# Four low-rank weight folds between two attentions: full-height matmuls, or four 32-row tiles side by side

## The reference, cut to what matters

```python
def _lora(t, down, up, alpha):
    return t @ down @ up * (LORA_W * alpha[0] / RANK)
q_in = x @ Wq + _lora(x, q_down, q_up, q_alpha)
org_ctx = context[:, :end, :]
ipa_ctx = context[:, end:, :]
k_in = org_ctx @ Wk + _lora(org_ctx, k_down, k_up, k_alpha)
v_in = org_ctx @ Wv + _lora(org_ctx, v_down, v_up, v_alpha)
out = _attention(q_in, k_in, v_in)
ipa_k = ipa_ctx @ Wk_ipa
ipa_v = ipa_ctx @ Wv_ipa
out = out + IPA_SCALE * _attention(q_in, ipa_k, ipa_v)
return out @ Wo + bo + _lora(out, o_down, o_up, o_alpha)
```

## Time and profile before

| what | value |
|---|---|
| median of three runs | 506.51 us (506.22, 506.51, 508.09) |
| the profiled execution | 506.04 us |
| its span, first to last instruction | 504.3 us |
| TensorE busy | 477.5 us, 95% |
| VectorE, ScalarE, GpSimd busy | 357.4, 292.7, 235.7 us |
| stretch of the seam, 99.6 to 129.4 us | 29.8 us |

### The profile page before, as it was taken

One profiled execution on the slowest core, in us unless ns is written; L12 is line 12 of the kernel. 1 busy time (PEld: TensorE's weight loads), 2 busy tenths in 40 slices (PEclk: granted clock), 3 DMA queues, 4 the chain that ended last, 5 costly groups with the idle time before them and its releaser, 6 DMA issues.

```text
span 504.3 us, 13570 instructions
## 1 busy us (share of the span) xinstructions
PE 477.5 (95%) x5109; PEld 376.4 (75%) x5113; DVE 357.4 (71%) x992; ACT 292.7 (58%) x1000; POOL 235.7 (47%) x331
## 2 busy tenths in 40 slices
PE   3999999999999999999999999799989999999996
PEld 2576666747678877888778777688757897899995
DVE  6788999787686668666686665857867779535553
ACT  3666656555676677666777657665674445513332
POOL 6664635145366554475544755233331990081430
PEclk9999999999999999999999999999999999999999
DMA  8900000000001110011000000022201200010001
GB/s 229 238 9 3 3 3 3 3 7 1 4 2 34 33 36 6 29 34 34 4 3 1 3 3 3 0 66 66 65 1 51 78 1 1 2 41 4 2 1 43
DMA packets 21872, 14.48 MB, mean 29 GB/s; under 512 B 5928, under 2 KB 21136, under 8 KB 21808
## 3 DMA queue, kind: packets, MB, share of 16 engines
q1 hardware_dynamic: 20704, 13.31, 9.9%
q10 hardware_dynamic: 1104, 0.30, 0.3%
HBM read 12.30 MB, written 1.05 MB: 26 GB/s over the span
## 4 chain that ended last, share of the span: by engine, by line
PE 69%; DVE 11%; issue 8%; POOL 5%; ACT 4%; DMA 1%; DVEq 0%; POOLq 0%
PE bank L1814 10%; PE bank L1758 6%; PE bank L1585 5%; PE bank L1823 5%; PE bank L1578 5%; PE bank L1565 5%; PE bank L1537 5%; PE bank L1490 5%; PE bank L1548 4%; PE bank L1557 4%; PE bank L1830 3%; POOL work L459 2%; ACT work L1184 2%; DVE work L792 2%; DVE negmax L782 2%
## 5 line engine op out<-in xcount | busy, mean ns | idle before, releaser
L497 POOL TENSOR_TENSOR work<-work,rsum 128x496 f32<-128x496 f32 x64 | 64.2, 1014 | 122.2 <-DVE rsum L798 122.2
L1184 ACT ACTIVATE work<-bank,negmax 128x124 f32<-128x124 f32 x256 | 90.4, 392 | 52.4 <-DVE ipa_s L784 52.3
L532 POOL TENSOR_SCALAR work<-work,slot 128x128 f32<-128x128 f32 x64 | 50.3, 801 | 44.6 <-DVE slot L873 25.7
L1184 ACT ACTIVATION_READ_ACCUMULATOR work<-bank,negmax 128x1 f32 x256 | 60.1, 235 | 0.0
L1814 PE MATMUL bank<-work 128*128 128x256 f32 x224 | 53.4, 381 | 0.0
L1333 ACT ACTIVATE work<-bank 128x256 f32<-128x256 f32 x64 | 24.6, 385 | 40.8 <-PE bank L1814 30.3
L1033 DVE SCALAR_TENSOR_TENSOR work<-work,bank 128x256 f32<-128x256 f32 x64 | 26.9, 420 | 28.7 <-ACT work L1333 28.3
L305 DVE TENSOR_TENSOR x_all<-bank,x_all 128x128 f32<-128x128 f32 x16 | 4.7, 292 | 56.8 <-PE bank L1758 54.8
L480 POOL TENSOR_TENSOR work<-work 128x512 f32<-128x512 f32 (+2 forms) x48 | 39.3, 818 | 11.8 <-DVE work L754 9.3
L629 DVE TENSOR_REDUCE work<-bank 128x8 bf16<-128x1024 f32 x32 | 39.0, 1220 | 7.6 <-PE bank L1375 7.2
L1814 PEld LDWEIGHTS bank<-work 128*128 128x128 f32 x224 | 40.3, 190 | 4.7 <-DVE work L1036 0.2
(11 more groups left out here) (199 smaller groups left out, 1104.0 us busy)
## 6 DMA issues: line engine op xcount, KB each, us to landing
work<-in_L_ffn_w_dram SPq DMA_DIRECT2D x42, 128.0 KB, 2.4
x_all<-in_x_dram SPq DMA_DIRECT2D x4, 256.0 KB, 5.9
out_dram<-x_all SPq DMA_DIRECT2D x4, 256.0 KB, 2.5
ctx_all<-in_ctx_dram SPq DMA_DIRECT2D x4, 192.0 KB, 6.0
ctx_all<-in_L_ffn_w_dram SPq DMA_DIRECT2D x6, 128.0 KB, 2.2
work<-in_L_xattn_Wq_dram SPq DMA_DIRECT2D x1, 512.0 KB, 6.5
work<-in_L_xattn_Wo_dram SPq DMA_DIRECT2D x1, 512.0 KB, 8.5
work<-in_L_ffn_We_dram SPq DMA_DIRECT2D x1, 512.0 KB, 6.6
```

The costliest lines, as they stand in the source:

```text
L497: pool.tensor_tensor(part, part, rsum1[:, b % 2, CH * n:CH * n + CH].unsqueeze(2).broadcast_to((128, CH, ORG)), ALU.mult).then_inc(Z.norm, 1)
L532: ins = pool.tensor_scalar(ohw_of(e)[:, k, :], count[:, :], slot[:, h, 0, k, e % E1:e % E1 + 1], slot[:, h, 1, k, e % E1:e % E1 + 1], ALU. ...
L1184: ins = act.activation(p1[:, b % 2, n, c, 0:ORG], blocks(bank[n])[:, c, 0:ORG], ACT.Exp, bias=negmax1[:, b % 2, h:h + 1], accum_out=sums1[ ...
```

## The change

The up matrices of o, q, k and v now lie under each other in one tile `ups` (rows 0, 32, 64, 96), the turned down matrices in the same rows of `downT`. `ext`, and the extra 32 rows of `wk1` and `wv1`, are gone. `fold_half(n)` makes half n of all four additions: three matmuls of 32 rows x 512 columns in row groups 1, 2 and 3 and four of 128 columns in row group 0, each into a bank of its own. VectorE adds all eight results to the weights (`added(n, name)`, semaphore `W.half` for ready, `W.added` for done); ScalarE's `take(0)` to `take(3)` fall away. `down_o_turn(0)` follows `down_turn` at b = 15, `down_o_turn(1)` stands at b = 16, `fold(6)` at b = 18. The loads change only in where the up matrices are put.

```diff
-            return slice(0, RANK) if n == 0 else slice(C, C + RANK)
-
-        FOLD_BANK = (0, 4, 5, 6, 0, 4, 0, 1, 2, 3, 4)
-        KEYS_TAKEN, VALUES_TAKEN, IPA_K_TAKEN, ALL_TAKEN = 2, 4, 5, 7
-        QUERIES_ADDED, ALL_ADDED = 2, 4
+            return slice(RANK * n, RANK * n + RANK)
+
+        O_ROWS = down_rows(0)
+        HALF_BANK = ({"q": 5, "k": 4, "v": 6, "o": 1}, {"v": 5, "q": 4, "k": 6, "o": 1})
+        HALF_ADDED = ({"q": 1, "k": 2, "v": 3, "o": 4}, {"v": 5, "q": 6, "k": 7, "o": 8})
+        FOLD_BANK = {6: 0, 7: 0, 8: 2}
+        IPA_K_TAKEN, ALL_TAKEN, ALL_ADDED = 1, 3, 8
...
-            def added(s, n):
-
-                to = (wq1[:, 512 * n:512 * n + 512], wo1[:, 4 * n:4 * n + 4, :].rearrange("p c n -> p (c n)"))[s >= 9]
-                dve.wait_ge(W.made, s + 1)
-                dve.tensor_tensor(to, bank[FOLD_BANK[s]][:, :], to, ALU.add).then_inc(W.added, 1)
+            def added(n, name):
+
+                part = slice(512 * n, 512 * n + 512)
+                rows = C if name in "kv" else D
+                to = wo1[:, 4 * n:4 * n + 4, :].rearrange("p c n -> p (c n)") if name == "o" else \
+                    {"q": wq1, "k": wk1, "v": wv1}[name][0:rows, part]
+                dve.wait_ge(W.half, 4 * (n + 1))
+                dve.tensor_tensor(to, bank[HALF_BANK[n][name]][0:rows, :], to, ALU.add).then_inc(W.added, 1)
...
-                if b == -1:
-                    added(9, 0)
-                    added(10, 1)
...
-                if b == 17:
-                    head_input(1)
-                if b == 18:
-                    added(4, 0)
-                    added(5, 1)
                 if b >= 17:
                     ffn_statistics(b - 17)
+                    added(b - 17, "qv"[b - 17])
                     xn1_of(b - 17)
+                if b == 17:
+                    added(0, "k")
+                    added(0, "v")
+                    head_input(1)
+                    added(0, "o")
+                if b == 18:
+                    added(1, "q")
+                    added(1, "k")
+                    added(1, "o")
...
-                act.wait_ge(made.ext, 1)
-                for n, to in enumerate((downT[:, 0, :], ext[C:C + RANK, 0, :], ext[C:C + RANK, 1, :])):
-                    rows = down_rows(n)
-                    act.activation(to, blocks(bank[0])[rows, n, 0:(D, C, C)[n]], ACT.Copy, scale=alpha[rows, n:n + 1])\
+                for n in range(3):
+                    rows, width = down_rows(1 + n), (D, C, C)[n]
+                    act.activation(downT[rows, 0, 0:width], blocks(bank[0])[rows, n, 0:width], ACT.Copy, scale=alpha[rows, n:n + 1])\
                         .then_inc(W.downT, 1)
 
             def down_o_turned(n):
 
                 act.wait_ge(W.turned, 2 + n)
-                act.activation(downT[:, 1 + 4 * n:5 + 4 * n, :], blocks(bank[(1, 6)[n]], RANK), ACT.Copy,
-                               scale=alpha[0:RANK, 3:4]).then_inc(W.downT, 1)
+                act.activation(downT[O_ROWS, 4 * n:4 * n + 4, :], blocks(bank[0])[O_ROWS, :, :], ACT.Copy,
+                               scale=alpha[O_ROWS, 3:4]).then_inc(W.downT, 1)
...
-                act.wait_ge(W.made, s + 1)
+                act.wait_ge(W.made, s - 5)
                 got_w = bank[FOLD_BANK[s]]
-                if s < 4:
-                    w, n = (wk1, wv1)[s // 2], s % 2
-                    to, got_w = w[0:C, 512 * n:512 * n + 512], got_w[0:C, :]
-                elif s == 6:
+                if s == 6:
...
                     down_turned()
+                    down_o_turned(0)
+                if b == 16:
+                    down_o_turned(1)
                 if b >= 16:
                     weighted(b - 16, bank[2])
-                if b == 16:
-                    take(0)
-                if b == 17:
-                    take(1)
-                    take(2)
-                    take(3)
                 if b == 18:
+                    take(6)
                     inputs(0)
-                    down_o_turned(0)
-                    down_o_turned(1)
...
+            def fold_half(n):
+
+                part = slice(512 * n, 512 * n + 512)
+                for r, (name, cols) in enumerate((("q", D), ("k", C), ("v", C))):
+                    rows = down_rows(1 + r)
+                    pe.matmul(bank[HALF_BANK[n][name]][0:cols, :], downT[rows, 0, 0:cols], ups[rows, part], start=True, stop=True)\
+                        .then_inc(W.half, 1)
+                for c in range(4):
+                    mm = pe.matmul(blocks(bank[HALF_BANK[n]["o"]])[:, c, :], downT[O_ROWS, 4 * n + c, :], ups[O_ROWS, 0:D],
+                                   start=True, stop=True)
+                mm.then_inc(W.half, 1)
...
                     pe.wait_ge(W.taken, IPA_K_TAKEN + 1)
+                    pe.wait_ge(W.added, ALL_ADDED)
...
-                if b == 0:
-                    pe.wait_ge(W.added, ALL_ADDED)
+                if b == -1:
+                    pe.wait_ge(W.added, HALF_ADDED[1]["q"])
...
-                    pe.wait_ge(W.added, ALL_ADDED - 1)
+                    pe.wait_ge(F.ys1, 3)
...
-                    pe.wait_ge(W.downT, 5)
+                    pe.wait_ge(W.added, HALF_ADDED[1]["k"])
                 if there(f):
                     keys(f, 0, *((Z.p_sb, CH * t + 2) if there(t) else (Z.v_sb, 2 * f)))
-                if b == -1:
-                    pe.wait_ge(W.added, QUERIES_ADDED)
-                    fold(6)
...
+                    pe.wait_ge(W.taken, IPA_K_TAKEN)
...
-                    pe.wait_ge(F.ys1, 3)
-                    fold(9)
-                    pe.wait_ge(Z.q_sb, 2)
-                    fold(10)
...
                     down_turn()
+                    down_o_turn(0)
                 if b == 16:
-                    pe.wait_ge(W.downT, 3)
-                    fold(0)
+                    pe.wait_ge(W.downT, 4)
+                    down_o_turn(1)
                 if b == 17:
                     pe.wait_ge(A.exp, 2 * B)
-                    fold(1)
-                    fold(2)
-                    fold(3)
+                    pe.wait_ge(A.o, B)
+                    pe.wait_ge(W.downT, 5)
+                    fold_half(0)
                 if b == 18:
-                    pe.wait_ge(W.taken, 2)
-                    fold(4)
-                    fold(5)
+                    fold(6)
+                    pe.wait_ge(W.added, 4)
+                    fold_half(1)
                     pe.wait_ge(A.x_new, B)
                     inputs(0)
-                    pe.wait_ge(A.o, B)
-                    down_o_turn(0)
-                    pe.wait_ge(W.taken, 4)
-                    down_o_turn(1)
-            pe.wait_ge(W.added, QUERIES_ADDED)
+            pe.wait_ge(W.added, HALF_ADDED[1]["v"])
```

40 lines of the change are left out of this document (13 added, 27 removed).

## The result

The changed kernel took 511.33 us (median of five executions, 508.14 to 511.95), the kernel before beside it 508.09 (506.22 to 508.52): ratio 1.0065, 95% interval 1.0044 to 1.0085. The forecast was 507.3, within 0.5% of before, and the range ended at 509.8; the result lies above it. The profiled execution took 510.95 us with a span of 509.1, 4.8 more than the 504.3 of before.

What follows compares the result with a forecast made beforehand. TensorE, busy 29.75 of the seam's 29.80 us, was taken as the bound. Its work, -5.3 us, plus waits of 2.05, 2.35, 0.8, 0.65 and 0.55 gave about +1.05 on 506.04: forecast 507.3 us, range 505.0 to 509.8.

Steps and rivals of the forecast that it cites:

- The folds and the tiles: TensorE in the seam: folds removed save 7.40 us, two fold_half at 1.05 add 2.1, net -5.3 us.
- the tiles don't overlap: At fold_half: tiles run one after the other, 3.4 us each, giving 509.4 to 510.8 us; chance 6%.
- TensorE's work decides: In the seam: VectorE and ScalarE keep up, 5.3 us gained, 500.7 us (503.9 with half the waits); chance 8%.
- Step 1: Ahead of ffn(1): TensorE waits for ScalarE's weighted(0), behind the copy of down_o_turn(1); idle 2.05 us.
- Step 3: Ahead of fold_half(1): TensorE waits until VectorE has added all four results of fold_half(0); idle 2.35 us.
- Step 4: Ahead of head_turn: TensorE waits for VectorE to add the first result of half 1; idle 0.8 us.
- Step 6: In ffn(3)'s second half: TensorE waits for ScalarE's weighted(3), with fold(6) gone from between; idle 0.55 us.
- Step 5: Ahead of ffn(3): TensorE waits for VectorE's first routing step, behind xn1_of(1) and three adds; idle 0.65 us.
- The sum: At scores(0, 0): -5.3 us of TensorE's work plus five waits, +1.1 us, the same as the walk's +1.05.
- the third rival: Idle 2.35 us ahead of fold_half(1) lowers the clock; half rate to ffn(3) adds 4.6 us, 511.7; chance 5%.
- signs of being wrong: First or second gap missing, a fold_half over 1.5 us, or the shift at scores(0, 0) not that at the end.
- Carried 1:1: From scores(0, 0) to the kernel's end: everything hangs on those scores, so the +1.05 us shift carries through in full.

Runs made afterwards that it cites:

- e12: Changed kernel with idle matmuls cut to the gaps: one ahead of ffn(1), two ahead of fold_half(1), two in round 12; 507.23 us, ratio 1.0007.
- e10: Kernel before with two idle matmuls filling TensorE's 1.45 us wait in round 12 of the second attention; 506.45 us, ratio 0.9986.
- e7: Changed kernel with VectorE's fourth add, added(0, o), put ahead of head_input(1); 508.94 us, ratio 1.0019.
- e6: Changed kernel with weighted(0) ahead of down_o_turned(1), fold(7) and fold(8) moved ahead of fold_half(1), and the fourth add ahead of head_input(1); 505.84 us, ratio 0.9965.
- e8: Kernel before with TensorE made to wait for two idle ScalarE copies behind fold(5), 1.38 us idle; 510.51 us, ratio 1.0066.
- e11: e6 with the idle matmuls of round 12 besides; 505.78 us, ratio 0.9976.
- e2: Changed kernel with four idle matmuls ahead of fold_half(1) only, the gap ahead of ffn(1) left idle; 508.39 us, ratio 1.0022.
- e3: Changed kernel with ScalarE's weighted(0) put ahead of down_o_turned(1); 506.53 us, ratio 0.9998.
- e4: Kernel before with TensorE made to wait for three idle ScalarE copies behind fold(5), 2.04 us idle; 511.66 us, ratio 1.0067.
- e1: Changed kernel with seven idle matmuls: three ahead of ffn(1), four ahead of fold_half(1); 508.60 us, ratio 1.0027.
- e5: Changed kernel with weighted(0) ahead of down_o_turned(1), and fold(7) and fold(8) moved ahead of fold_half(1); 506.35 us, ratio 0.9978.

## Why the prediction was wrong, point by point

**What bounds the seam** held: TensorE was full, and work taken from it came back as waits for ScalarE and VectorE.

**The folds and the tiles** held. The tiles overlap: a fold_half takes 1.11 us, predicted 1.05. Of the rivals, *the tiles don't overlap* (3.4 us each) is out, and so is *TensorE's work decides*: the 5.3 us were not gained.

**The waits** were found in the right places, with the right releasers, each somewhat too long. Step 1: 1.77 measured, 2.05 predicted. Step 3: 2.09 and 2.35. Step 4, with the clock kept (e12): 0.65 and 0.8. Step 6: 0.34 and 0.55. Step 5's wait is not marked in e12; the distance from L1560 to ffn(3) is 1.20 us (120.70 to 121.90) against 0.98 before, so 0.2 and not 0.65. A likely reason is that I counted from the starts of instructions and added about 0.1 us for each handover on top of durations that already hold some of it.

**The sum** of +1.05 us was right in sign and a little large: with the clock held, +0.43 at the first scores in one profile and +0.78 by the medians of e12 and e10. That e12 measures 507.23 us where 507.3 was forecast is partly luck: its 0.78 stands on 506.45 (e10), the forecast's 1.05 on the 506.0 to 506.5 known then. What the Trainium skill says of reading PSUM (TensorEngine Tiling (Array Packing), "PSUM Bottleneck") agrees with the traces in part: VectorE's adds, not the tiles, set when fold_half(1) may start (2.09 us). But the adds are only 2.6 of the 5.0 us that VectorE needs; the wait is as much a matter of what stands between them, for it is 0.91 with one add moved ahead (e7) and gone with other work in it as well (e6).

**The reading of the earlier trace rows** as the lower of TensorE's two levels is not what the granted clock says: the table by windows of before has 1.00 from 16 to 20 us, though two passes take 0.64 us there. What the lower level does to lengths is shown by the changed kernel instead, at 0.50 (1.12 us for 0.60).

**The step that failed** is the clock, which the sum put at nothing and the third rival at 5%. *The clock falls in the gap* was written down with its place, its mechanism and its price. It is what happened, in the gap ahead of fold_half(1), and it costs 3.6 of the 4.05 us that the seam lost. That the rival's 511.7 us lies so near the measured 511.33 is largely luck: it stands for +5.65 (1.05 + 4.6) on 506.04, where the seam lost 4.05 (0.43 + 3.62) and the two medians differ by 3.24. (Three of the five executions of before beside it, at 508.09 and more, lie where the later ones with a mean clock of 0.996 lie.) The price of 4.6 also rests on half rate for the work up to ffn(3); in the profile the lower clock stands longer, for some 10 us, and costs less, since part of it falls where TensorE would have waited anyway: the waits of steps 5 and 6 are not in that profile. The 5% had no ground. The earlier trace rows are one execution with 1.45 us of idle time and no fall, and the prediction itself says that they don't show what 2.35 us does. One of the three times that I had (506.22 to 508.09) lies where later executions with a mean clock of 0.996 lie, and I did not ask why. e7's profile shows that the very gap of the earlier trace rows can lower the clock, and by e8's mean clocks 1.38 us at the seam does it in most executions. The range ended at 509.8 since it left out this rival. None of the prediction's own signs of being wrong came true, for none of them asks for the clock.

**Carried 1:1** held for the loss (4.79 of 4.8 us of span), and not for a gain: e11 gives part of its 2.77 us back.

Open: why a gap lowers the clock in one execution and not in the next, why the 1.77 us ahead of ffn(1) lowered it in none of the three profiles that have them (the changed kernel, e2, e7) while 2.1 us did, and why it stays low for some 3.5 us in e3 and e7 and for some 10 in e4 and the changed kernel. Nor is it the same moment: by the table in steps of half a microsecond it falls in the middle of the gap in e4 (at 115.2, the gap ending at 116.1), but 0.9 us behind the gap's end in the changed kernel, 1.4 behind it in e7 and 1.7 in e3. The Trainium skill (TensorE: Matmul & The Clock Gate, Part 1) says that what watches TensorE's activity runs freely and does not restart with the kernel; by that the same gap would meet it at another moment in every execution, which fits the two groups of before and these moments, but no run here tests it. Open too is the one execution of the changed kernel at 508.14 us, whose mean clock (0.991) is as low as that of the others; there is no trace of it.

## What to carry to other kernels

An idle time of 1.4 to 2.1 us on a full TensorE could cost more than itself here: up to about 4 us more, by the granted clock behind it, and in some places and executions nothing more. So before folding work away from a saturated TensorE, look which waits that work was hiding, and put other needed work into the gap (e6) rather than leave it empty, watching where the next gap opens (1.86 us in e11); even idle matmuls were better than nothing (e1, e2, e12). And look at the granted clock of several executions, not of one: a gap that one profile shows to be harmless may be what spreads the times of the next.

## What the runs showed of the hardware

- TensorE's granted clock fell from 1.00 to 0.50 at idle times of 2.09 us (the changed kernel), 2.10 (e3), 2.04 (e4) and 1.46 (e7, round 12), in one profile each. By the mean clocks of all executions, most of them without a trace, it fell in at least four of six with 2.04 us and three of five with 1.38, and in about a third of before's with 1.45, if that is what sets its two groups apart; at 0.72 us nothing clearly beyond the fall known from before was seen.
- Idle times of the same length also left it at 1.00: 1.77 us ahead of ffn(1) in three profiles of three, 1.85 to 1.86 us in three (e5, e6, e11), 1.38 us in e8's, and 1.45 us in round 12 in ten of the eleven that have it.
- While it stands at 0.50, four turns take 1.12 us for 0.60, sixteen score matmuls 1.90 for 1.16.
- Four 32-row tiles, three wide and one made of four narrow matmuls, take 1.11 us side by side, hardly more than the 0.95 of one alone.
